# Key, value and query projections by half batches over eight PSUM banks, and a new order of the attention tiles

## The reference, cut to what matters

```
x += tanh(g0) * cross_attention0(layernorm(x), ctx)        # 16 heads, 64 context rows
x += tanh(g1) * moe(layernorm(x))                          # 16 experts, best 4 per row, one shared expert
x += tanh(g2) * attention1(layernorm(x), mem=ctx)          # causal, 16 heads of 16, keys = ctx rows + x rows
x += tanh(g3) * quantised_dense(layernorm(x))
```

```
q = x @ Wq
kv = concatenate((mem, x), axis=1) @ Wkv; k, v = split(kv)
dots = einsum('bhid,bhjd->bhij', q, k) * scale; mask j > i + mem_len
out = softmax(dots) @ v; return out @ Wout + bout
```

## Time and profile before

| | |
|---|---|
| median of three runs | 1586.02 us |
| the profiled execution's own time | 1576.49 us |
| its span, first to last instruction | 1574.8 us |
| busy: PE, DVE, ACT, POOL | 70%, 65%, 40%, 30% of the span |
| mean granted TensorE clock | 0.844 of full |

### The profile page before, as it was taken

How to read it: one execution, slowest core, us unless ns; L and a number is a source line. 1 busy time by engine, 2 the same in 40 slices (tenths; PEclk the granted TensorE clock), 3 DMA queues, 4 the chain that set the end, 5 groups by cost and what they waited for, 6 DMA issues and landing times. The chain is left out here.

```text
span 1574.8 us, 23905 instructions
## 1 busy us (share of the span) xinstructions
PE 1102.2 (70%) x8155; PEld 568.3 (36%) x8155; DVE 1020.3 (65%) x1857; ACT 635.4 (40%) x1273; POOL 478.3 (30%) x540
## 2 busy tenths in 40 slices
PE   3799984233319999404445658898989898988867
PEld 2355552122106666201222312333333333332546
DVE  4899875535346766344545467888888878880575
ACT  0455652111103333100211306677677776776330
POOL 1334232776740000377456151111111111111010
PEclk7999997665559999756767758999999999998888
DMA  6010100222279999633545631211111112100003
GB/s 201 21 32 29 40 1 30 87 83 84 97 242 237 256 255 255 200 96 99 167 138 160 190 81 37 61 50 37 38 57 53 37 38 62 48 2 1 1 0 107
DMA packets 183649, 146.24 MB, mean 93 GB/s; under 512 B 102638, under 2 KB 160494, under 8 KB 183546
## 3 DMA queue, kind: packets, MB, share of 16 engines
q1 hardware_dynamic: 164906, 103.79, 25.2%
q0 software_dynamic: 12288, 33.57, 6.5%
q10 hardware_dynamic: 6352, 7.48, 1.4%
HBM read 53.11 MB, written 68.55 MB: 77 GB/s over the span
## 5 line engine op out<-in xcount | busy, mean ns | idle before, releaser
L1703 DVE TENSOR_REDUCE small<-ps 128x2 f32<-128x960 f32 (+6 forms) x384 | 383.3, 1042 | 65.6 <-PE ps L1757 63.7
L1682 ACT ACTIVATE region<-ps 128x512 f32<-128x512 f32 (+5 forms) x768 | 343.4, 533 | 119.4 <-PE ps L1771 117.9
L1771 PE MATMUL ps<-region 50*128 50x512 f16 (+5 forms) x896 | 194.4, 328 | 41.0 <-ACT region L1682 40.1
L1653 POOL TENSOR_SCALAR_AFFINE_SELECT region<-region 128x512 f32<-128x512 f32 (+2 forms) x160 | 87.7, 548 | 443.4 <-ACT region L1682 443.4
L1843 PE MATMUL ps<-region 128*32 128x512 f32 (+5 forms) x1792 | 189.9, 497 | 7.3 <-POOL region L1653 6.6
L852 POOL DMA_INDIRECT expert_rows<-region,small x128 | 132.1, 1032 | 69.6 <-issue 36.6
L1757 PE MATMUL ps<-region 48*128 48x480 f16 (+6 forms) x896 | 148.7, 335 | 5.5 <-DVE small L1703 4.4
L1193 PE MATMUL ps<-region 128*128 128x384 f16 x696 | 125.1, 331 | 29.2 <-DMA region<-expert_rows 28.9
L1316 POOL DMA_INDIRECT region<-result_rows,home x128 | 129.1, 1009 | 37.6 <-issue 37.6
L1771 PEld LDWEIGHTS ps<-region 50*128 50x128 f16 (+1 forms) x896 | 54.0, 95 | 180.2 <-ACT region L1682 154.8
L1442 PE MATMUL ps<-region 128*128 128x512 f16 (+1 forms) x240 | 57.3, 406 | 63.0 <-DVE region L1400 46.1
(11 more groups left out here) (233 smaller groups left out, 1688.2 us busy)
## 6 DMA issues: line engine op xcount, KB each, us to landing
result_rows<-region SPq DMA_DIRECT2D x58, 384.0 KB, 4.0
v_parts<-region SPq DMA_DIRECT2D x16, 576.0 KB
region<-v_parts SPq DMA_DIRECT2D x16, 576.0 KB, 3.9
region<-k_parts SPq DMA_DIRECT2D x96, 68.0 KB, 2.2
region<-q_parts SPq DMA_DIRECT2D x96, 64.0 KB, 2.1
k_parts<-region SPq DMA_DIRECT2D x16, 272.0 KB
x_sb<-in_x ACTq DMA_DIRECT2D x8, 512.0 KB, 9.5
region<-in_w13T SPq DMA_DIRECT2D x16, 256.0 KB, 2.9
```

What stands on the lines that cost most here:

```text
L1653: nc.gpsimd.affine_select(out=t, in_=t, compare_op=ALU.is_ge, fill=0.0, base=r0, pattern=[[0, G], [1, w]], channel_multiplier=-1).then_inc ...
L1682: nc.scalar.activation(dst, src, ACT.Exp, scale=SCALE).then_inc(s_exp, 1)
L1703: nc.vector.tensor_reduce(nmp[:, qt, :, p0:p0 + np_, place], s_pair(n + first)[:, :, 0:np_ * nk] .rearrange("p e (h k) -> p e h k", h=np_) ...
L1771: ins = nc.tensor.matmul(o, ka[rr, tbuf, pair, kt * P:kt * P + rows], qa[rr, tbuf, pair, q0:q0 + nq], start=True, stop=True)
```

## The change

It has three parts.

1. In routing, for chunk 6 alone, Pool makes a small power of four columns between the eighth and the ninth scatter and waits for its end.
2. The projections are rewritten by chunks. All eight PSUM banks are used in turn (`turn`, `bank`, `moved`). A first chunk of a batch yields q00 q10 k00 k10 and the values of two pairs of tiles; a second q01 q11 k01 k11 k02 k12 and the other four value products. DVE's order is `combine(c, 0)`, `x_low(c - 1)`, `combine(c, 1)`, `statistics(c)`, `low(c - 1)`, `normalised(c)`. The copies of the context move from Pool to ACT. Pool's gathers stay 16 per chunk with the reciprocal root between the two parts, and nothing between the second part of a chunk and the first of the next. SP's loop is unrolled. The counts of products, copies and stores are the same.
3. `ORDER` of the second attention has the same items in another sequence.

```diff
+                        elif j == TC // 2 and c + 1 < CHUNKS:
+                            nc.gpsimd.tensor_tensor(pause4[:], half[:], half[:], ALU.pow).then_inc(s_break, 1)
+                            pool.wait_ge(s_break, 1)
...
-            ring = Ring([(f"x{k}{h}", "dve") for h in range(2) for k in range(KH)] + [(n, "dve") for n in QN + KN] +
-                        [(f"v{n}", "act") for n in range(len(VT))])
+            SPLITS = (("q00", "q10", "k00", "k10"), ("q01", "q11", "k01", "k11", "k02", "k12"))
+            VALUES = ((0, 1), (2, 3, 4, 5))
+            order = [(c, n, "act" if n[0] == "v" else "dve") for c in range(2 * B) for n in
+                     [f"x{k}{c % 2}" for k in range(KH)] + list(SPLITS[c % 2]) + [f"v{i}" for i in VALUES[c % 2]]]
+            turn = {(c, n): i for i, (c, n, _) in enumerate(order)}
...
+            def bank(c, name):
+
+                return turn[c, name] % 8
...
-                    if c == 2:
-                        pool.wait_ge(s_wsplit, 1)
-                    if c and c % 2 == 0:
-                        context(c // 2 - 1)
                 ln_pool(nc.gpsimd, 2 * B - 1, s_var, s_rstd)
-                context(B - 1)
...
+                    if h == 1 and b + 1 < B:
+                        context(b + 1)
...
-                for h in range(2):
-                    normalise(order, 0, h)
-                for b in range(B - 1):
-                    batch(b, True)
-                batch(B - 1, False)
+                for c in range(2 * B):
+                    combine(c, 0)
+                    if c:
+                        x_low(c - 1)
+                    combine(c, 1)
+                    statistics(c)
+                    if c:
+                        low(c - 1)
+                    normalised(c)
+                x_low(2 * B - 1)
+                low(2 * B - 1)
...
+                def wait_free(c, name):
+                    if turn[c, name] >= 8:
+                        wait_moved(turn[c, name] - 8)
...
+                    wait_moved(turn[c, f"x1{h}"])
+                    pe.wait_ge(s_wsplit, 1)
+                    for name in SPLITS[h]:
...
-        ORDER = """T2 PV0 T3 S9 PV1 T4 S10 T5 PV2 S11 T6 S12 T7 PV3 S13 T8 S14 T9 PV4 S15 T10 S16 PV5 T11 S17 PV6
-                   T12 S18 T13 PV7 S19 T14 S20 T15 PV8 S21 T16 S22 T17 PV9 S23 T18 T19 PV10 T20 mT0 N0 T21 PV11
-                   N1 T22 N2 T23 N3 PV12 N4 N5 PV13 Tn0 N6 Tn1 N7 N8 oT0"""
+        ORDER = """T2 PV0 T3 S9 PV1 T4 S10 T5 S11 PV2 T6 S12 T7 PV3 T8 S13 S14 T9 PV4 T10 S15 S16 PV5 T11 S17 PV6
+                   T12 S18 T13 S19 PV7 T14 S20 T15 PV8 T16 S21 S22 T17 PV9 T18 S23 T19 PV10 T20 mT0 N0 T21 PV11
+                   T22 N1 T23 N2 N3 PV12 N4 PV13 N5 Tn0 N6 Tn1 N7 N8 oT0"""
```

More of the change, by code:

```diff
@@ L1280, in _ @@
                     sp.dma_start(dst, src.rearrange("(k p) n -> p k n", p=P)).then_inc(s_in, 16)
-                with sp.Fori(0, B) as b:
-                    hold(sp, s_pstored, (b + 1) * P_STORES + 1, s_tick)
+                for b in range(B):
+                    sp.wait_ge(s_pstored, (b + 1) * P_STORES + 1)
                     for parts, dram, name in ((qp, q_parts, QN[-1]), (kp, k_parts, KN[-1])):
-                        hold(sp, s_dve, ring.moved(b, name)[1], s_tick)
+                        sp.wait_ge(s_dve, moved(turn[2 * b + 1, name]))
                         for part in range(PARTS):
@@ L1339, in _, with context @@
                 nc.scalar.activation(ch[:], c_sb[:], ACT.Copy).then_inc(s_whigh, 1)
-                for b in range(B):
-                    for h in range(2):
[L1342 to L1347, removed]
+                def context(b):
+                    nc.scalar.activation(xch[:, :, 0:CTX], ch[:, :, b * CTX:(b + 1) * CTX], ACT.Copy)
+                    nc.scalar.activation(xcl[:, :, 0:CTX], cl[:, :, b * CTX:(b + 1) * CTX], ACT.Copy).then_inc(s_ctx, 1)
@@ new lines, in _ @@
+                act.wait_ge(s_wsplit, 1)
+                context(0)
+                for c in range(2 * B):
+                    b, h = c // 2, c % 2
+                    for k in range(KH):
+                        act.wait_ge(s_full, full(c, f"x{k}{h}"))
+                        nc.scalar.activation(xch[:, k, CTX + h * CH:CTX + (h + 1) * CH], ps[:, bank(c, f"x{k}{h}"), :],
+                                             ACT.Copy).then_inc(s_xhigh, 1)
+                    if h == 0:
+                        act.wait_ge(s_pstored, b * P_STORES + 1)
+                    for name in SPLITS[h]:
@@ L1354, in _ @@
-                    for n, (t0, nt) in enumerate(VT):
+                                             ps[:, bank(c, name), 0:size], ACT.Copy, scale=1.0 / WS).then_inc(s_high, 1)
+                    if h == 0:
+                        act.wait_ge(s_vstored, b * V_STORES + 1)
+                    for n in VALUES[h]:
+                        t0, nt = VT[n]
                         rows = P if t0 < KT - 1 else KEYS - (KT - 1) * P
-                        act.wait_ge(s_full, ring.full(b, f"v{n}"))
+                        act.wait_ge(s_full, full(c, f"v{n}"))
@@ L1396, in batch, with low @@
+                def low(c):
+                    for i, name in enumerate(SPLITS[c % 2]):
                         m, n = int(name[1]), int(name[2])
                         off, size = KCH[n]
-                        high, low = (part_of(name, b, part, m, slice(off, off + size)) for part in range(PARTS))
-                        dve.wait_ge(s_high, b * N_SPLIT + i + 1)
-                        nc.vector.scalar_tensor_tensor(out=low, in0=ps[:, ring.bank(name), 0:size],
+                        high, low_ = (part_of(name, c // 2, part, m, slice(off, off + size)) for part in range(PARTS))
+                        dve.wait_ge(s_high, c // 2 * N_SPLIT + (c % 2) * len(SPLITS[0]) + i + 1)
+                        nc.vector.scalar_tensor_tensor(out=low_, in0=ps[:, bank(c, name), 0:size],
@@ L1401, in batch @@
                                                        scalar=1.0 / WS, in1=high, op0=ALU.mult,
                                                        op1=ALU.subtract).then_inc(s_dve, 1)
-                    if more:
-                        normalise(order, b + 1, 1)
-                    assert not more or order.n == SELF
                 dve.wait_ge(s_whigh, 1)
@@ L1445, in _ @@
-                        pe.full(ins)
-                    for n, (t0, nt) in enumerate(VT):
-                        pe.wait_free(b, f"v{n}")
+                            for wt, xt in three:
+                                ins = nc.tensor.matmul(ps[:, bank(c, name), 0:size], wt[:, kh, w0 + m * P:w0 + (m + 1) * P],
+                                                       xt[:, kh, x0:x0 + size], start=i == 0, stop=i == 5)
+                                i += 1
+                        ins.then_inc(s_full, 1)
@@ L1448, in _ @@
+                    for n in VALUES[h]:
+                        t0, nt = VT[n]
+                        wait_free(c, f"v{n}")
                         for t in range(t0, t0 + nt):
```

130 lines of the change are left out of this document (65 added, 65 removed).

## The result

| | before | changed |
|---|---|---|
| median of 12 runs each | 1586.19 us | 1571.1 us (1560.83 to 1581.1) |
| ratio to the kernel before | 1 | 0.9921, 95% interval 0.9899 to 0.9942 |
| the profiled execution's own time, span | 1576.49, 1574.8 us | 1566.55, 1564.7 us |
| routing: the last scatter starts at | 459.36 | 458.61 |
| experts end, projections begin | 652.80 | 656.74 |

By the ratio the change is faster by 0.8%, 12.5 us; the two medians lie 15.1 us apart. 39 us were forecast. The ledger of the two profiled executions is +3.9 (experts) - 7.8 (projections) + 0.8 - 7.2 (second attention) + 0.1 = -10.1 us, the difference of the spans. The forecast for this sum was -38.6, so 28.5 us are missing. 21.8 of them are missing in the projections, where 29.6 us were forecast with the slow signals counted.

A forecast was written before the change was run, and what follows sets the result against it. Projections were taken as bound by POOL's 128 gathers plus 40.5 us of waits and a tail, second attention near PE's limit. Terms -39.6 + 10 - 3 - 6 = -38.6 us gave 1537.9, forecast 1547 us with the median's offset; range 1528 to 1580.

The forecast's parts named there:

- the slow signal: Projections: PE's signals reach ACT late while POOL issues gathers; one stop taken, +10 us, ends 0 and 48.
- The rival that was given 0.24: Projections: signals hold POOL up in every batch, three stops of 11 us, 33 in place of 10, 1570 us; chance 0.24.
- The prediction's own sign: Projections: the forecast is wrong if POOL stops for 12 us or more in two or more places.
- The three waits go: Projections: with variances ahead of the low parts, POOL's three waits before the root vanish, 40.5 us off.
- The pace: Projections: POOL's roots follow every 22.14 us from 687.87, the seventh at 820.7.
- The tail: Projections, after the last gather: landing 1.8, variances 5.3, root 1.2 us, then half a batch of products; stage ends at 863.
- Routing: Routing: Pool's pause in chunk 6 shortens its wait before chunk 7; -3 us, at most 4.6 gained.
- The attention's order: Second attention: the new order cuts PE's waits by 0.45 us per unit, -6 us, of a 20 us bound.
- DVE and POOL in each other's way: Projections: DVE's multiply-adds slow 104 gathers by 0.33 us each, 34 us, giving 1581 us; chance 0.04.
- The copies on ACT and the stores: Projections: context copies moved to ACT and SP's stores cost nothing; the copies at most 4.8 us without cover.
- The profiled execution: Whole kernel: the median of the runs lies 9.5 us above the profiled execution, added to 1537.9 us.

The follow-up runs named there:

- e8: The kernel before with a small power on Pool and a wait for its end behind each sixteen gathers of the projections, nothing else changed; 1566.46 us, ratio 0.9906.
- e1: The changed kernel with a small power on Pool and a wait for its end behind each sixteen gathers of the projections; 1549.38 us, ratio 0.9791.
- e2: The changed kernel with a pause of Pool behind every four gathers of the projections, the reciprocal root counting as one; 1566.07 us, ratio 0.9897.
- e12: The changed kernel with pauses behind each sixteen gathers and, in routing, one more pause ahead of the first scatter of chunk 6; 1542.1 us, ratio 0.978.
- e11: The kernel before with the new order of the second attention and nothing else; 1571.09 us, ratio 0.9937.
- e6: The changed kernel with Pool waiting for the end of each reciprocal root before the next gather, no added pauses; 1562.72 us, ratio 0.9903.
- e4: The changed kernel without Pool's pause in routing; 1566.61 us, ratio 0.99.
- e9: The changed kernel with a memset of one element per partition, without a wait, behind each sixteen gathers of the projections; 1559.51 us, ratio 0.9864.
- e10: The changed kernel with the projections' 128 gathers replaced by 128 plain loads on SP, so the rows added are not the chosen experts'; 1476.13 us, ratio 0.9339.

## Why the prediction was wrong

1. **The step that failed** is the size of the slow signal: "I take one stop, of 10 us (nearest to the shorter ones, 11.96 us), because DVE is late only where several signals are late in one row". There were three stops, 10.19, 4.67 and 13.08 us, 27.9 in all: 17.9 us more than the term, out of the 21.8 us that the projections lacked. The rival that was given 0.24, three stops of 11 us and 1570 us, is what happened: 1571.1. The prediction's own sign, 12 us or more in two places, did not appear; it was set too coarse for shorter stops. The mechanism had been read rightly from ACT's rows; what was not drawn from it was its share in the stops of before.
2. **What went before it**: "The three waits go: 40.5 us off". The order of DVE's rows was taken as the cause of the whole wait. e8 shows that with DVE's order as it was, pauses alone bring the two real stops from 28.5 to 2.5 us. The cause was the same late signal, so the new order alone did not remove it; with the pauses in both kernels the new order's projections are 8.6 us shorter (e1 against e8). The third wait of 11.96 us was never a stop but the tail; it is 10.50 us in the changed kernel.
3. **The pace** was right where nothing stops POOL: e1's seventh root came 1.4 us from the schedule with the seven pauses counted.
4. **The tail**, from the seventh root to the end of the stage, was forecast at 863 - 820.7 = 42.3 us, and was 53.9 before; it measured 898.69 - 851.99 = 46.7. So 7.2 us were won in place of 11.6. The step was the landing of 1.8 us and the variances of 5.3 behind the last gather, 7.1 us: POOL waited 10.50 us there, 3.4 of the 4.4 us. In the changed kernel `x_low` of chunk 6 came late once more by a signal, in front of the last `combine`. In e2, where no signal is late, DVE got the last rows at 863.40, 4.6 us behind the last gather (857.88 + 0.95), with SP's stores of values from 849.59 on just ahead; that these stores delay it was not tried.
5. **Routing**, forecast -3 us: the last scatter is 0.75 us earlier in the pair of profiles and 3.8 us in the means over thirteen, but DVE's wait stayed, since the pause came behind the row of sixteen that held the signal (eight scatters of chunk 5, eight of chunk 6); e12's pause between these eights took it to 4.66 us. No gain in time could be measured.
6. **The attention's order**, forecast -6 us out of 0 to 20: the mechanism was right and the size somewhat small; e11 measured 10 us (0.9923 to 0.9951), half of the bound of 20, and the pair of profiles shows 7.2.
7. **DVE and POOL in each other's way**: in the projections a gather's issue took 1019 ns in the mean, 1009 before: 1.3 us over all 128, where the rival had 34. The rival falls.
8. The copies on ACT and the stores cost nothing that can be seen, as taken. The profiled execution lay 4.5 us under the median, not 9.5.

The Trainium skill (Perfetto Trace Analysis, Summary: the profiler window per engine type) says that the propagation of a semaphore is in no engine's window and that TensorE's ends are estimates. The trace agrees in kind: PE's rows end at 734.3, the wait on them at 738.84, and only the waiting engine's "<-remote" shows it. Which of the two hidden things took the 4.5 us, no run here shows, and the page's table gives no length for either.

## What to carry to other kernels

Ask of every wait whether its releaser was late by its own work or by a wait of its own: follow it back until a row has a cause that the profile names, and ask there what the other engines were issuing: "<-remote", or "<-issue" on PE, was in this kernel where the cause stood. Where one engine issues long rows of indirect transfers, try a break of about a microsecond of that engine's own work every eight before reordering the others; every four cost more here than it gave (242.6 us for 224.2). And leave the last wait of a stage out of the sum of its stops; it has another cure.

## What the runs showed of the hardware

Where Pool issued sixteen indirect transfers without other work between them (one each 1.25 us for gathers, 1.27 us for scatters), what waited for PE's products went on late; the longest waits were 15.62 us of ACT (e6) and 21.52 us of DVE in routing (e4):

```profile
735.19 1.09 ACT L1377 ACTIVATE region<-ps 128x512 f32<-128x512 f32 x2 [15.62 <-remote]
```

In such rows PE itself gave one product per 1.4 to 2.1 us. With a power of 1.05 us between each eight the longest such wait of ACT was 4.1 (e12) to 9.5 us (e1), with one between each four there was none (e2). A wait on a semaphore behind a root added nothing (e6); a memset of 0.1 us took away at most a part (e9). As many bytes by plain loads on SP, at 225 in place of 146 GB/s, left no wait of ACT without a local cause (e10). What in the chip connects Pool's gathers with PE's products and signals, no run here shows.
